# A causal attention layer whose projections for head pairs 1 to 3 move into the attention loop, with plain float32 scores

## The reference

```python
hx = _layernorm(x, ln_g, ln_b)
q = (hx @ Wq).reshape(b, n, h, dh).transpose(0, 2, 1, 3)      # h = 8 heads of dh = 64
k = (hx @ Wk).reshape(b, n, h, dh).transpose(0, 2, 1, 3)
v = (hx @ Wv).reshape(b, n, h, dh).transpose(0, 2, 1, 3)
q = _l2norm(q) * scale * qn_g                                 # x / sqrt(sum(x^2) + eps), per head
k = _l2norm(k) * scale * kn_g
scores = jnp.einsum('bhqd,bhkd->bhqk', q, k) * dh ** (-0.5)
scores = jnp.where(causal, scores, jnp.finfo(scores.dtype).min)
attn = jax.nn.softmax(scores, axis=-1)
o = jnp.einsum('bhqk,bhkd->bhqd', attn, v)
```

## Time and profile before

| what | value |
|---|---|
| median of 3 runs | 1664.78 us (1664.73 to 1671.17) |
| the profiled execution, its own time | 1665.02 us |
| its span in the trace | 1663.2 us |
| mean granted TensorE clock | 0.968 |
| front of the causal layer in the trace | 231.8 to 372.4 us |
| attention of the causal layer in the trace | 372.4 to 605.4 us |

### The profile page before, as it was taken

The page is one execution under the profiler, slowest core; times in us unless marked ns, Lnnn a source line. Parts: engine busy times, 40 slices in busy tenths (PEclk is TensorE's granted clock), DMA queues, the critical chain, the costliest instruction groups (busy, mean ns, idle before and its releaser), DMA issues. The chain is left out here.

```text
span 1663.2 us, 22381 instructions
## 1 busy us (share of the span) xinstructions
PE 1473.0 (89%) x8224; PEld 923.3 (56%) x8224; DVE 1017.1 (61%) x1890; ACT 726.9 (44%) x1404; POOL 634.2 (38%) x517
## 2 busy tenths in 40 slices
PE   3888977997787889999999899877999999998998
PEld 1554533446666654454545554446676676776654
DVE  5998143327777721113123322855999999999994
ACT  4452013324555531101101230053778778878774
POOL 3788100015656410000000042004966766766763
PEclk8999989998999998999999999989999999999999
DMA  6001000035222041000000110003011011011001
GB/s 235 1 2 80 0 1 1 0 67 156 43 54 45 20 160 72 0 0 1 1 0 0 36 40 0 1 1 89 1 33 33 1 33 33 1 33 33 2 1 63
DMA packets 28621, 57.04 MB, mean 34 GB/s; under 512 B 7952, under 2 KB 12692, under 8 KB 28256
## 3 DMA queue, kind: packets, MB, share of 16 engines
q1 hardware_dynamic: 27200, 53.03, 11.6%
q10 hardware_dynamic: 1312, 2.56, 0.4%
HBM read 28.77 MB, written 5.84 MB: 21 GB/s over the span
## 5 line engine op out<-in xcount | busy, mean ns | idle before, releaser
L1324 POOL TENSOR_TENSOR tl_ex<-tl_ex,tl_left 128x1250 f32<-128x1250 f32 x80 | 209.9, 2624 | 36.0 <-ACT tl_left L1642 32.0
L1161 DVE SCALAR_TENSOR_TENSOR X<-ex_ps_x,g,X 128x512 f32<-128x512 f32 x80 | 59.9, 750 | 192.6 <-PE ex_ps_x L1054 192.6
L1450 PE MATMUL tl_banks<-identf,tl_ex 128*128 128x128 f32 x800 | 136.5, 285 | 22.4 <-ACT tl_pt L1663 11.2
L1956 POOL TENSOR_TENSOR lo<-xn,hi 128x512 f16<-128x512 f32 x5 | 5.9, 1188 | 379.6 <-ACT hi L2046 379.6
L1027 PE MATMUL ex_ps_h<-yt,w 128*128 128x512 f32 (+1 forms) x384 | 144.1, 529 | 0.0
L1054 PE MATMUL ex_ps_x<-w,hid 128*128 128x512 f32 (+1 forms) x320 | 143.1, 599 | 0.0
L1663 ACT COPY tl_pt<-tl_banks 128x512 f32<-128x512 f32 (+1 forms) x200 | 108.3, 541 | 79.0 <-PE tl_banks L1450 75.5
L1450 PEld LDWEIGHTS tl_banks<-identf,tl_ex 128*128 128x128 f32 x800 | 89.0, 142 | 85.6 <-issue 44.7
L1107 ACT ACTIVATE hid<-ex_ps_h,b 128x512 f32<-128x512 f32 (+1 forms) x48 | 29.1, 608 | 242.4 <-PE ex_ps_h L1027 242.3
L1738 DVE MAX8 tl_m<-tl_banks 128x8 f32<-128x1250 f32 x80 | 116.4, 1455 | 5.6 <-PE tl_banks L1427 5.6
L1744 DVE MAX8 tl_m<-tl_left 128x8 f32<-128x1250 f32 x80 | 117.1, 1464 | 2.8
(11 more groups left out here) (280 smaller groups left out, 2990.6 us busy)
## 6 DMA issues: line engine op xcount, KB each, us to landing
kl<-KT SPq DMA_DIRECT2D x16, 320.0 KB, 4.3
qs<-QO SPq DMA_DIRECT2D x16, 320.0 KB, 5.7
tl_kl<-tl_KT SPq DMA_DIRECT2D x16, 320.0 KB, 4.3
tl_qs<-tl_QO SPq DMA_DIRECT2D x16, 320.0 KB, 5.8
w<-in_L_ffn_W SPq DMA_DIRECT2D x8, 512.0 KB
w<-in_L_ffn_W SPq DMA_DIRECT2D x4, 1024.0 KB, 9.0
at_kept<-AT SPq DMA_DIRECT2D x1, 3200.0 KB, 9.0
AT<-at_kept SPq DMA_DIRECT2D x1, 3200.0 KB, 18.9
```

The lines of the kernel that those rows point to most:

```text
L1324: pool.tensor_tensor(ex[:, n % EXS, 0:N], ex[:, n % EXS, 0:N], left[:, n % LEFT, :], ALU.subtract).then_inc(s_probs, 1)
L1450: mm = pe.transpose(ps_t[:, b * P:(b + 1) * P], ex[:, n % EXS, a + b * P:a + (b + 1) * P], m.identf[:, :])
```

## The change

Only `causal_layer` changes.

1. **Jobs.** The projections are cut into 40 jobs, a head pair by a tile: `project(j)` makes queries, keys and values of one pair for one tile in 4 matmuls of 384 columns. The ten jobs of pair 0 and three of pair 1 (AHEAD = 13) run in the front. The other 27 run in the attention: job j is projected by PE at the end of step n = 2(j-13), an even step from 0 to 52; ACT copies it out of PSUM in step n+1 (`keep_raw`, two copies); POOL squares it; DVE sums it in step n+2; ACT takes the root and DVE scales it in step n+3; PE transposes it and ACT keeps it in step n+4. All tiles' transposed inputs stay in memory (`ht`).
2. **Banks.** Banks 6 (jobs) and 7 are taken, so up to unit 53 every group of transpositions goes through bank 5 alone and waits for the copy of the group just before it. Later groups alternate again.
3. **Scores.** Queries and keys stay float32. `scores(n)` is two (three for tile 9) float32 matmuls of half the partitions each, one part of the keys on partitions 0 to 63 and another on 64 to 127, in different banks. SP makes the swapped copies per pair; `stage` is gone.
4. **Order and sharing.** PE interleaves transpositions with scores; `keep` on DVE and ACT moves; DVE normalises tiles 9, 8 and 7 only and POOL the rest.
5. **Loads.** The expert weights are issued after the fourth pair's copies.

```diff
             def root(t):
...
+            def root(j):
+                act.wait_ge(s_summed, j + 1)
+                act.activation(ss[:, j % RAWS, 1, :], ss[:, j % RAWS, 0, :], ACT.Sqrt, bias=m.eps[:, 1:2]
+                               ).then_inc(s_root, 1)
...
             for n in range(TN + LAG + 1):     # ACT
+                keep(n - LAG, 0)
                 if 0 <= n - 1 < TN:
                     exponentials(n - 1)
+                if n - 1 in unit_at and n - 1 >= 0:
+                    keep_raw(unit_at[n - 1])
+                if n - 3 in unit_at and n - 3 > -4:
+                    root(unit_at[n - 3])
+                if n - 4 in unit_at:
+                    keep_qk(unit_at[n - 4])
+                keep(n - LAG, 1)
                 if n - LAG - 1 in pair_of:
                     keep_o(pair_of[n - LAG - 1])
-                if 0 <= n - LAG < TN:
-                    keep(n - LAG)
+                keep(n - LAG, 2)
...
+            def project(j):                   # PE
+                i, t = place(j)
...
+                elif j >= AHEAD:
+                    pe.wait_ge(s_raw, j)
+                    pe.wait_ge(s_qk_kept, j - 1 if j == AHEAD else j - 1)
                 for k in range(KD):
+                    mm = pe.matmul(banks[:, job_bank(j), 0:3 * P].rearrange("p (n c) -> p n c", n=3),
+                                   ht[:, t, k, :], wqkv[:, :, k, i * P:(i + 1) * P],
                                    start=(k == 0), stop=(k == KD - 1))
...
             for n in range(TN + LAG + 1):     # PE
+                turn(n - LAG, 0)
                 if n < TN:
                     scores(n)
+                if n - 4 in unit_at:
+                    turn_qk(unit_at[n - 4])
+                turn(n - LAG, 1)
                 if n - LAG - 1 in pair_of:
                     weigh(pair_of[n - LAG - 1])
-                if 0 <= n - LAG < TN:
-                    turn(n - LAG)
+                turn(n - LAG, 2)
+                if n in unit_at:
+                    project(unit_at[n])
...
             for n in range(TN + LAG + 1):     # DVE
                 if n < TN:
                     largest(n)
+                if 0 <= n - LAG < TN:
+                    keep(n - LAG)
+                if n - LAG - 1 in pair_of:
+                    keep_o(pair_of[n - LAG - 1])
                 if 0 <= n - 1 < TN:
                     invert(n - 1)
-                    if (n - 1) % 2 == 0:
+                    if scaled_by[n - 1] == "dve":
                         normalise(n - 1)
...
+                if n - 2 in unit_at and n - 2 >= 0:
+                    sums(unit_at[n - 2])
+                if n - 3 in unit_at and n - 3 > -4:
+                    unit(unit_at[n - 3])
```

More of the change, by code:

```diff
@@ L605, in _, with squares @@
         def _(pool):
[L606 to L626, removed]
+            def squares(j):
+                pool.wait_ge(s_raw, j + 1)
+                if j >= SQS:
+                    pool.wait_ge(s_summed, j - SQS + 1)
+                pool.tensor_tensor(sq[:, j % SQS, :], raw[:, j % RAWS, :], raw[:, j % RAWS, :], ALU.mult
+                                   ).then_inc(s_sq, 1)
             def normalise(n):
@@ new lines, in _ @@
+            turn_x(0)
+            turn_x(1)
+            for j in range(AHEAD):
+                project(j)
+                if j + 2 < NT:
+                    turn_x(j + 2)
+                if j >= 2:
+                    turn_qk(j - 2)
+            def scores(n):
+                h, t = n // NT, SEQ[n % NT]
+                i = h // 2
+                pe.wait_ge(s_fetched[i % 2], 64 * (i // 2 + 1))
+                if n < 2:
+                    pe.wait_ge(s_qk_kept, WHOLE)
+                else:
+                    pe.wait_ge(s_exp, n - 1)
+                for half, a, b in parts(n)[1]:
+                    r = slice(half * DH, (half + 1) * DH)
+                    q, k = (QO[r, i, :], KT[r, i, :]) if half == h % 2 else (qd[r, i % 2, :], kd[r, i % 2, :])
+                    mm = pe.matmul(logits(n)[:, a:b], q[:, t * P:(t + 1) * P], k[:, a:b], start=True, stop=True)
+                    if half == 1 or a > 0:
+                        mm.then_inc(s_scored, 1)
@@ L795, in _, with keep_raw @@
[L795 to L799 removed]
+            def keep_raw(j):
+                i, t = place(j)
+                act.wait_ge(s_qkv, j + 1)
+                if j >= RAWS:
+                    act.wait_ge(s_qn, j - RAWS + 1)
+                act.copy(raw[:, j % RAWS, :], banks[:, job_bank(j), 0:2 * P])
+                act.copy(V[:, t, i * P:(i + 1) * P], banks[:, job_bank(j), 2 * P:3 * P]).then_inc(s_raw, 1)
@@ L801, in exponentials @@
+            act.wait_ge(s_gained, 1)
+            for t in range(3):
+                normed(t)
+            for j in range(AHEAD):
+                keep_raw(j)
+                if j + 3 < NT:
+                    normed(j + 3)
+                if j:
+                    root(j - 1)
+                if j >= 2:
+                    keep_qk(j - 2)
             def exponentials(n):
```

336 lines of the change are left out of this document (146 added, 190 removed).

## The result

The changed kernel takes 1756.3 us (median of four runs, 1753.8 to 1758.1) against 1666.3 us for the kernel before on the same chip: 1.053 times the time, 95% interval 1.051 to 1.056. The forecast was 1720 us, range 1690 to 1762. The direction and the mechanism hold; the size was forecast at +55 us and is +90.

What follows compares the result with a forecast made beforehand. A closed line of PE's job, transpositions and ACT's list with two table loads bounds the attention, 11.0 us a pair; its end moves from 605.7 to 660.5 us, +55 us on 1665.0, so 1720 us, range 1690 to 1762.

Steps and rivals of the forecast that it cites:

- The front: Projections before the attention: first scores at 285.1 us instead of 372.4, giving back 87 us.
- The line through ACT: Attention, steps 0 to 52: job, transpositions and ACT's whole list follow one another without overlap, 11.0 us a pair of steps.
- The loads' part: Two table loads per pair in ACT's line, for root and exponentials, 1.31 us a switch, 13.0 us a head.
- the faster rival: Attention: tables don't switch or ACT is not in the line; 8.4 us a pair, 1652 us in all; chance 0.07.
- together 54.8 a head, 11.0 a pair of steps: Attention's job steps: ACT's list 35.6, PE's part 16.6 and small waits 2.6 us a head; 283 us from job 13 to 39.
- PE's part in the line: job 2.58: Attention, each pair: job 2.58, transpositions 0.69, hand-over 0.05, so 3.3 us, five times 16.6 a head.
- the small waits: Attention: small units' transpositions wait for ACT's copy from bank 5, and weighings hold jobs back; 2.6 us a head.
- The last units: Attention after job 39: 26 units at 2.78 us; last roots' loads add 3, interleaved order saves about as much; end 660.5.
- the forecast's own case: Attention's job steps at 10.3 to 12.0 us a pair, 1702 to 1746 us in all; chance 0.71.
- the halves running in turn: Scores in the attention: the two halves don't run side by side, 5.8 us a head more, 1736 us; chance 0.14.
- No drain: Rival on ACT: a drain of 1.38 us more at every switch from root to exponential, 1795 us; chance 0.04.
- The expert loads: Moved to start after step 56 of the attention, some 80 us ahead of their use: no cost.

Runs made afterwards that it cites:

- e2: The changed kernel with the keep of a job's keys and queries put ahead of the same step's exponentials in ACT's queue: 1740.1 us, ratio 1.041.
- e1: The changed kernel with Identity instead of Sqrt for each job's root, so tables need not switch and norms are left out: 1697.0 us, ratio 1.019.
- e9: The changed kernel with Identity for Sqrt, ACT's keep of keys and queries ahead of the exponentials, and DVE scaling all big units: 1694.8 us, ratio 1.016.
- e5: The changed kernel with six spare transpositions on PE ahead of the job in 17 of the steps: 1742.5 us, ratio 1.044.
- e10: The changed kernel with only the sharing undone, so DVE scales every big unit, tiles 6 and 5 again: 1745.5 us, ratio 1.046.
- e7: The changed kernel with both parts of each score on the same half of the partitions, so they can't run side by side: 1838.6 us, ratio 1.102.
- e12: The changed kernel with all 40 jobs in the front, DVE scaling all big units, and both score parts on one half: 1694.3 us, ratio 1.015.
- e3: The changed kernel with all 40 projection jobs in the front and transpositions back on two banks: 1674.1 us, ratio 1.000.
- e6: The changed kernel with Ln and Exp on ACT in place of Sqrt and DVE's reciprocal: 1842.2 us, ratio 1.104.
- e8: The changed kernel with all 40 jobs in the front, two transposition banks, and DVE scaling every big unit: 1649.3 us, ratio 0.988.

## Why the prediction was right in its sign and short in its size

- **The front** was right to 1.1 us: the first scores at 284.0, against 285.1.
- **The line through ACT** was right, with its members and its releaser. e2 changes nothing but an order on ACT and gains 16 us; e1 takes the loads out of it and gains 59. The loads' part, 26 x 2.6 = 68 us, was too high: a pair without them takes 9.8 us, not 8.4, and the 26 pairs get 47.9 us shorter, a part of it by faster jobs. Below some 10 us another limit stands; the waits of e9 for copies and keep are the likely one. So the faster rival would not have been faster: with the tables held, the kernel takes 1697 us, not 1652.
- **The step that failed** is "together 54.8 a head, 11.0 a pair of steps", and in it the term "PE's part in the line: job 2.58". It priced the job at 2.4 GHz. Measured are 58.0 a head and 302.1 us over 26 pairs, where the sum had 283: 19 us. Jobs at 1.2 GHz are 16.8, from their busy time; e5 brings 15.9 of them back. That this nearly fills the 19 is in part luck, for other terms were off in both directions. Over the four heads from 334.4 us, ACT's own work in the line is 34.4 us a head (forecast 35.6), PE's part with the hand-overs 19.3 (16.6; 2.1 of the excess are slow jobs), and the small waits 4.3 (2.6). The prediction counted how long PE waits in each pair and not what the wait does to the work behind it. It had the row for a warning: the first projections of the front run slowly after a wait, 2.5 us of the forecast.
- **The last units** were the second failure, "26 more units at 2.78 ... the interleaved order saves about as much". From job 39 to the next stage it took 101.5 us (691.8 - 590.3), and the prediction had 89.5: 12 us. DVE's smaller share was not costed at all. In it POOL's scaling of big tiles makes PE wait (7.3 us in all), and the clock is 0.90. e10 gives DVE these tiles back and gains 11, of which 8.9 lie in this part.
- **The sum again.** The attention was to end 54.8 us later than before (660.5); with 19.3 for the jobs and 12.0 for the last units it is the measured 86.1. The pace, 11.6 us a pair, lies in the forecast's own case (10.3 to 12.0), but the total lies above its 1746; the upper part of the range was there for the halves running in turn, which did not happen. That 1756 is inside the range is partly luck.
- **No drain, and the halves side by side**: both rivals are excluded, the one by the timeline, the other by the timeline, e7 and e12. The second was priced far too low, at 16 us (1736); e7 has it at 82. **The expert loads** were free, as forecast; no wait for them shows in the stages behind.

What stays open: what lowers the clock where PE waits little (0.77 in e7 with PE busy 84%, 0.91 in e12 with 93%), and why e3 and e2 have runs 16 to 20 us apart at clocks that differ by 0.01. How much of the price of a job, and of e9's remainder, is the single bank for the transpositions was not tried: no run parts the bank from the jobs.

## What to carry to other kernels

Before work is moved into the gaps of another loop, follow it through each in-order queue: where an engine's job waits for a keep that stands behind that same engine's next product, the gaps are part of a closed line and that job can't fill them. Count the switches of ScalarE's tables that the new order makes, and take TensorE's work in a line with waits at a lower clock than the trace of before shows. Try each part of such a change alone: here the projections all in the front (and with them two banks for the transpositions), the half-array scores, and the big tiles' scaling left on DVE give 1649 us, 1.2% faster than before, out of a change that as a whole is 5.3% slower.

## What the runs showed of the hardware

- TensorE given more work finished earlier: 102 spare transpositions made the kernel 14 us faster, through a clock of 0.93 instead of 0.88.
- Two float32 matmuls on the two halves of the partitions start within 0.01 us of each other and run side by side; that is worth 45 us of 1694 (e12), a part of which is the clock's. Each record has about 0.11 us that doesn't shrink with its width, by an estimate from spacings of 0.27 us for 192 keys and 0.54 for 512.
- A switch between Exp and Sqrt costs 1.3 us from the end of one instruction to the start of the next. Ln and Exp, used in turn, switch as well (e6, two loads of 1.28 us a job).
- The clock can fall where TensorE hardly waits: with both parts of the scores on one half it was 0.91 with PE busy 93% of 273.0 us (e12), against 0.99 with 86% (e8).
- With one program and one chip the clock has more than one course: e3 took 1674 us three times and 1654 us once.
